# Two local-attention layers and their feed-forwards, written as one unrolled stream of 32 tile steps

## The reference

```python
x = x + _L0_xattn_ref(ctx_768, layernorm(x), mask, ...)   # A: 2 heads of 64, 256 + 256 keys
x = x + _L0_ffn_ref(layernorm(x), ...)                    # B: two layers of the following
x = x + _L1_xattn_ref(layernorm(x), ctx_768, ...)         # C: 8 heads of 64, 256 keys
x = x + _L1_ffn_ref(layernorm(x), ...)                    # D: gated feed-forward with fake quantisation

def _layer(x, wqkv, qs, ksc, wo, lg, lb, w1, b1, w2, b2):  # one layer of B
    q, k, v = split(shift_token(x) @ wqkv)                # 8 heads of 64
    q, k = rotary_xpos(l2norm(q) * qs, l2norm(k) * ksc)
    x = x + local_attention(q, k, v) @ wo
    h = layernorm(shift_token(x)) * lg + lb
    a, g = split(h @ w1 + b1)                             # 2 x 341 columns
    return x + (a * gelu(g)) @ w2 + b2
```

## Time and profile before

| | |
|---|---|
| median of 3 runs | 1018.42 us (1013.97 to 1022.93) |
| span of the profiled execution | 1025.1 us |
| PE busy (share of the span) | 870.8 us (85%) |
| PEld, DVE, ACT, POOL busy | 539.7, 665.1, 539.1, 386.2 us (53, 65, 53, 38%) |
| A, B, C and D in the profiled execution | 0 to 184.7, to 743.7, to 971, to 1025.1 us |

### The profile page before, as it was taken

The page is one execution under the profiler, slowest core; times in us unless marked ns, Lnnn a source line. Parts: engine busy times, 40 slices in busy tenths (PEclk is TensorE's granted clock), DMA queues, the critical chain, the costliest instruction groups (busy, mean ns, idle before and its releaser), DMA issues.

```text
span 1025.1 us, 17045 instructions
## 1 busy us (share of the span) xinstructions
PE 870.8 (85%) x4931; PEld 539.7 (53%) x4931; DVE 665.1 (65%) x1935; ACT 539.1 (53%) x1490; POOL 386.2 (38%) x476
## 2 busy tenths in 40 slices
PE   2898889699999998795999999987989999999642
PEld 1344444355565566563555555564656666666411
DVE  3755663467777777554577777765556666667566
ACT  1445552346666666422466666663256566555252
POOL 5634452655555554114565555621000111110102
PEclk9879995769999999998699999999999999999765
DMA  6400000000000000101000000000000000000001
GB/s 187 92 1 1 0 0 0 1 1 1 1 1 0 0 0 1 44 2 24 0 0 0 0 0 0 0 0 0 1 1 1 2 0 0 0 0 1 1 1 41
DMA packets 16492, 10.40 MB, mean 10 GB/s; under 512 B 6612, under 2 KB 15390, under 8 KB 16351
## 3 DMA queue, kind: packets, MB, share of 16 engines
q1 hardware_dynamic: 16446, 9.90, 3.8%
HBM read 8.84 MB, written 1.05 MB: 10 GB/s over the span
## 4 chain that ended last, share of the span: by engine, by line
PE 31%; DVE 11%; issue 5%; ACT 3%; POOL 1%; DVEq 0%; POOLq 0%; ACTq 0%
PE PS L655 8%; PE PS L665 5%; PE PS L685 4%; PE PS L707 3%; PE PS L741 2%; PE PS L759 2%; PE PS L849 2%; DVE mx L1161 2%; PE PS L766 1%; PE PS L749 1%; DVE rsin L1259 1%; DVE ss L1262 1%; PE PS L762 1%; PE PS L858 1%; ACT pb L950 1%
## 5 line engine op out<-in xcount | busy, mean ns | idle before, releaser
L655 PE MATMUL PS<-big 64*128 64x192 f32 (+3 forms) x832 | 216.8, 387 | 0.8 <-ACT big L1004 0.8
L655 PEld LDWEIGHTS PS<-big 64*128 64x128 f32 x832 | 129.0, 196 | 55.8 <-issue 52.2
L1161 DVE TENSOR_REDUCE mx<-PS 128x2 f32<-128x384 f32 (+3 forms) x192 | 122.7, 639 | 39.3 <-PE PS L655 37.7
L541 POOL TENSOR_TENSOR rot<-rot,rsin 128x512 f32<-128x512 f32 x64 | 83.7, 1308 | 162.0 <-DVE rsin L1259 161.9
L741 PE MATMUL PS<-wqkv,hB 128*128 128x512 f32 x192 | 113.8, 693 | 27.9 <-ACT hB L989 18.7
L1009 ACT ACTIVATE pT<-PS 128x512 f32<-128x512 f32 x192 | 115.0, 599 | 20.4 <-PE PS L665 20.4
L685 PE MATMUL PS<-pT,V 128*64 128x128 f32 x1280 | 108.5, 292 | 11.9 <-ACT pT L1009 9.7
L685 PEld LDWEIGHTS PS<-pT,V 128*64 128x64 f32 x1280 | 68.8, 139 | 86.7 <-issue 70.1
L1179 DVE RECIPROCAL rden<-den 128x2 f32<-128x2 f32 (+2 forms) x192 | 31.2, 162 | 117.3 <-ACT pb L950 53.4
L665 PE MATMUL PS<-ident,pb 128*128 128x128 f32 x512 | 88.6, 299 | 3.9 <-DVE pb L1188 3.8
L996 ACT ACTIVATE sq<-PS 128x512 f32<-128x512 f32 x64 | 38.2, 597 | 86.8 <-PE PS L741 86.3
(11 more groups left out here) (217 smaller groups left out, 1596.4 us busy)
## 6 DMA issues: line engine op xcount, KB each, us to landing
wqkv<-in_L_ffn_wqkv SPq DMA_DIRECT2D x2, 768.0 KB, 4.6
out<-x SPq DMA_DIRECT2D x4, 256.0 KB, 2.3
x<-in_x SPq DMA_DIRECT2D x1, 768.0 KB, 5.4
ctxT<-in_ctxT SPq DMA_DIRECT2D x1, 768.0 KB, 7.5
w<-in_L_ffn_w SPq DMA_DIRECT2D x2, 341.0 KB
ctxs<-in_ctx SPq DMA_DIRECT2D x1, 576.0 KB, 6.5
woB<-in_L_ffn_wo SPq DMA_DIRECT2D x8, 64.0 KB, 3.8
x<-in_x SPq DMA_DIRECT2D x1, 256.0 KB, 2.8
```

What stands on the lines that cost most here:

```text
L541: tt(rot[:, m, :], rot[:, m, :], rsin[:, is_q, :], ALU.add).then_inc(sem("B_sum"), 1)
L655: i = mm(bank[:, n * nk:(n + 1) * nk], q, k, start=(ph == "C"), stop=(ph == "C" or n == len(heads) - 1))
L1161: red(m, PS[:, SB + s % 2, 0:nh * nk].rearrange("p (n k) -> p n k", n=nh), AXX, ALU.max) \
```

## The change

Only B is written anew; A, C and D keep their code. The loop over layers, the loop over batches, the units, pieces and the separate feed-forward of B go. In their place every engine has one straight list of 47 steps: tile n (0 to 31: two layers of 16 tiles) enters at step n, and each engine's part of it follows at a fixed lag.

- **Scores.** All 8 heads of a tile stand in two banks at once. Each window of 64 queries meets 128 keys: its own 64 and the 64 before. So a head takes two matmuls of 64 contraction rows, 64 stationary columns and 128 moving ones, 16 per tile, and the two masks are 512 columns each.
- **Softmax.** One maximum over 128x1024, one subtraction of it over 128x1024 (DVE), one exp over 128x1024 (ACT), eight transposes back into the same two banks, one copy of 128x1024 (ACT). Nothing is divided there: V has a 65th column of ones, so that the value sum brings the row sum with it, and DVE divides the 512 outputs.
- **Values.** The turned probabilities are stationary (64 columns), V moves (65 columns), 16 matmuls per tile. The outputs come out by tokens, so four transposes (L870) and a copy are added. The first window's keys are mixed from two tiles by one or two DMAs from SBUF to SBUF (`mixed_values`).
- **q and k.** POOL takes the 16 inverse norms in one power and scales both q and k.
- **Feed-forward.** Group g's steps lie at steps 4g+7 to 4g+13 between the attention's, with one pair of banks for its three up-chunks, so each chunk waits for the gelu and the gate of the one before. The shifted half comes by three DMAs (`shifted_half`), and POOL adds `b2`.
- **Loads.** Both layers' weights are loaded at the start, layer 1's into `xy`, which was free until C. The scales `xeff` of both layers are made in A's last batch.
- PE, ACT and POOL's B parts start when all of `y` is ready; C starts on PE after the last residual of B.

```diff
-            with pe.Fori(0, DEPTH) as layer:
-                pe.wait_ge(sem("ld_wqkv"), layer * 112 + 112)
...
-                attention("B", layer, between=lambda: f_shift(0))
...
+            def b_scores(n):
+                pe.wait_ge(sem("B_qT"), n + 1)
+                pe.wait_ge(sem("B_kT"), n + 1)
+                if n >= 1:
+                    pe.wait_ge(sem("B_pT"), n)
+                j = n % 2
+                for r in range(2):
+                    mm(PS[:, BS + r, :], identb[:], (band_b if j else band_a)[:], start=True, stop=False)
+                for c in range(4):
+                    for w in range(2):
+                        for r in range(2):
+                            rows = slice(r * DH, (r + 1) * DH)
+                            keys = kTB[rows, n // 2 % 2, c, j * P + w * WINDOW:j * P + w * WINDOW + P]
...
+                            i = mm(PS[w * WINDOW:(w + 1) * WINDOW, BS + r, c * P:(c + 1) * P],
+                                   qTB[rows, n % 2, c, w * WINDOW:(w + 1) * WINDOW], keys, start=False, stop=(c == 3))
+            def b_values(n):
...
+                for k, h in enumerate(HEADS):
+                    for w in range(2):
+                        v = vown[:, n % 3, h, :] if w else vmix[:, n % 2, h, :]
+                        i = mm(PS[w * WINDOW:(w + 1) * WINDOW, BO + k // 4, k % 4 * 65:(k % 4 + 1) * 65],
+                               pTB[n % 2][:, k, w * WINDOW:(w + 1) * WINDOW], v, start=True, stop=True)
+            for i in range(LAST_STEP + 3):          # PE; its order within a step
+                up01, up2, down, ft = group_at(i, 11), group_at(i, 12), group_at(i, 13), group_at(i, 10)
...
+                    f_up(up01, 0)
...
+                    b_project(i, 0, BP).then_inc(sem("B_q"), 1)
...
+                    f_down(down)
...
+                    f_up(up2, 2)
...
+                    b_turn_outputs(i - 4)
...
+                    f_turn(ft)
+                if 2 <= i < NT + 2:
+                    b_scores(i - 2)
...
+                    f_up(up01, 1)
...
+                    b_project(i, 1, BP + 1).then_inc(sem("B_k"), 1)
...
+                    b_output(i - 4)
+                if 3 <= i < NT + 3:
+                    b_values(i - 3)
...
+                    b_turn(i + 1)
...
+                    b_turn_qk(i - 1, 1, BP).then_inc(sem("B_qt"), 1)
...
+                    b_project(i, 2, BK).then_inc(sem("B_v"), 1)
...
+                    b_turn_qk(i - 1, 0, BP + 1).then_inc(sem("B_kt"), 1)
+                if 2 <= i < NT + 2:
+                    b_turn_probs(i - 2)
...
+            for i in range(LAST_STEP + 3):          # DVE; POOL and ACT have lists of the same kind
+                if 3 <= i < NT + 3:
+                    b_max(i - 3)
...
+                    f_gate(g, 2)
...
+                    b_residual(i - 5)
...
+                    f_gate(g, 1)
...
+                    b_rotate(i - 1, 0)
+                    b_sum_squares(i - 1, 0)
...
+                    b_divide(i - 4)
...
+                    b_sum_squares(i - 1, 1)
...
+                    f_stats(g)
...
+                    b_rotate(i, 1)
```

More of the change, by code:

```diff
@@ L141, in over_batches, with values_landed, group_at @@
     body(B - 1, 1, "last")
+def values_landed(n):
+    return 16 * (1 + n % 2) * (n // 2 + 1)
+def group_at(i, first):
+    g, r = divmod(i - first, 4)
+    return g if r == 0 and 0 <= g < GROUPS else None
 def wait(eng, sem, value):
@@ L398, in ffn_weights @@
                              "ld_w12")
[L399 to L404, removed]
-            later_loads()
[L406 to L410, removed]
-                sp.wait_ge(sem("y_ready"), layer * B + B + FIRST)
-                ffn_weights(layer)
+                load(lnB[:, layer, 0:1], t_in["L0_ffn_ln_g"][layer].rearrange("(n o) -> n o", o=1), "ld_w12")
@@ new lines, in _ @@
+            pool.wait_ge(sem("ld_w12"), DEPTH * 12 * 16)
+            for i in range(LAST_STEP + 2):
+                if 1 <= i <= NT:
+                    b_add(i - 1, 0)
+                if (g := group_at(i, 12)) is not None:
+                    f_bias(g)
+                if (g := group_at(i, 8)) is not None:
+                    f_copy(g)
+                if 1 <= i <= NT:
+                    b_roots(i - 1)
+                    b_scale(i - 1, 1)
+                    b_scale(i - 1, 0)
+                if (g := group_at(i, 8)) is not None:
@@ L803, in attention @@
                     turn_probs(ph, u, s)
-                    if s == n - 2 and between:
-                        between()
                     if ph != "A" or s % 2:
@@ new lines, in _, with b_tokens, b_square @@
+            act.wait_ge(sem("B_pad"), 2)
+            def b_tokens(n):
+                act.wait_ge(sem("B_xt"), n + 1)
+                at, bank = hB[:, n // 2 % 2], PS[:, BK + 1, 0:P]
+                j = n % 2
+                af(at[0:DH, j * P:(j + 1) * P], bank[0:DH], ACT.Copy)
+                af(at[DH:D, j * P + 1:(j + 1) * P + 1], bank[DH:D], ACT.Copy).then_inc(sem("B_hB"), 1)
+            def b_square(n, w):
+                act.wait_ge(sem("B_%s" % "kq"[w]), n + 1)
+                wait(act, sem("B_ss%d" % w), n)
+                af(sqB[w], PS[:, BP + 1 - w, :], ACT.Square).then_inc(sem("B_sq%d" % w), 1)
@@ L1325, in body @@
                         dve.wait_ge(sem("ln_rstd"), 6)
-                    if ph == "B":
-                        dve.wait_ge(sem("B_rs"), layer * (4 * B) + b * 4 + 4)
+                    if ph == "A" and where == "last":
+                        xpos_scales()
                     for s in range(n):
@@ new lines, in b_residual, with f_stats @@
+            def b_residual(n):
+                dve.wait_ge(sem("B_wo"), n + 1)
+                yt = y[:, n % T, :]
+                tt(yt, PS[:, BP, 0:D], yt, ALU.add).then_inc(sem("B_ya"), 1)
+            def f_stats(g):
+                dve.wait_ge(sem("B_fc"), g + 1)
+                dve.wait_ge(sem("B_fs"), (g + 1) * 48)
+                for j in range(4):
+                    i = nc.vector.bn_stats(bstf[:, j, :], hs[:, j, :])
+                then(i, "B_fbn", g + 1)
+                for j in range(4):
+                    i = nc.vector.bn_aggr(mvh[:, j, :], bstf[:, j, :])
+                i.then_inc(sem("B_hst"), 1)
```

711 lines of the change are left out of this document (397 added, 314 removed).

## The result

| | before | after |
|---|---|---|
| median, us | 1020.67 (4 runs, 1013.97 to 1033.21) | 895.09 (4 runs, 893.98 to 902.80) |
| span of the profiled execution, us | 1025.1 | 892.5 |
| B, from its first block on PE to C's first | 559.0 | 432.9 |

The ratio is 0.879 with an interval of 0.873 to 0.886: faster, by 126 us. Now and then an execution runs longer at a lower granted clock throughout (the worst here is one of an experiment, 1156.9 us at 0.65, beside 943.4 at 0.91), and the ratios leave such executions out. The forecast was 931 in a range of 890 to 990. The range held; the gain was 1.4 times the 87 us forecast.

The account below looks back on a forecast made before the run. PE was taken as the bound. 32 tiles at 11.4 (365), feed-forward 67, fill 15 and drain 18 make B 465 us, ending 89 earlier; less 2 for seams, 87 saved: 938 profiled, 931 median, range 890 to 990.

Parts of the forecast that it names:

- B's start: First block of B on PE: it waits for all of `y`, finished by POOL, so B begins at 189.5 us.
- the seams: Where B meets A and C: 2 us taken off the 89 us gain, leaving 87.
- The mechanism: In B, PE bounds the stream: 13.5 us per tile with feed-forward, against at most 9.7 on any other engine.
- PE per tile, 10.6 and 0.8 for waits: Attention in B: PE's blocks sum to 10.6 us per tile, plus 0.8 idle: 11.4, against 13.7 before.
- The rival of the four quarters: Scores and values in B both run at their lower ends, 1.6 us less per tile: 886 us; chance 0.13.
- The feed-forward, 8.4 per group: Feed-forward within B's stream: PE works 8.4 us for each of eight groups, 67 us in all.
- Fill and drain, 33: Start and end of B's stream: 15 us to fill, paid once instead of twice, and 18 to drain.
- The DMAs, costed at nothing: Transfers of mixed V and the shifted half in B land in time, at no cost; 2 us late per group costs 16.
- POOL, DVE, ACT: Other engines in B, per tile with feed-forward: POOL 9.7, DVE 9.3, ACT 8.2 us, below PE's 13.5.
- The rival of late chains: Power, table loads or the probabilities' copy are late in B, some 1.6 us per step: +50, 981 us; chance 0.17.
- The drains: PE must empty between array quarters, so 64 small-matmul rows per tile pay 0.17 each: +237, 1168 us; chance 0.05.
- The clock: Short waits keep the granted clock low: B's 465 us become 552, no gain, at 0.79; chance 0.02 within 1%.

Follow-up runs that it names:

- the version without the stall: Feed-forward statistics, their inverse root and application one step later than in the changed kernel, nothing else: median 854.35 us, 0.834 of the kernel before, B 386.4 us.

## Why the prediction was right, and where it was off

On the profiled executions 938 was forecast and 892.5 came. Of the 45.5 us, 13.3 are B's start (189.5 forecast, 176.2 measured) and 32.1 its length (465 against 432.9); the 2 us taken off for the seams were right (283.4 behind B in place of 281.4). By the prediction's own steps:

- **The mechanism: right.** PE's work per tile sets the stream, and no other engine does. Without the stall PE is busy 99% of a period, and changes of 0.49, 0.75 and 1.46 us per tile came out as 13.5 to 14.2, 23.8 and 46.9 us.
- **PE per tile, 10.6 and 0.8 for waits: too high.** A plain step is 8.73 us. Scores were taken at 1.9 and measured 1.03, close to the lower bound of 0.9. Values were taken at 1.6 and measured 1.08, close to theirs of 1.0. The waits of 0.8 were not there. These three make 2.2 of the 2.7; the remaining half microsecond is spread over blocks that had rows. Eight transposes start 0.87 before the next block (207.97 to 208.84; forecast 0.98), and a projection 0.86 (208.84 to 209.70; forecast 0.955). In the third step, which has no wait, the four transposes of the outputs and both masks take 1.02 from start to start (1.19 forecast). Over 32 tiles: 279 us in place of 365.
- **The rival of the four quarters: it came true.** The choice was "the value rows' 0.053", since no row of before showed both halves of the rows at work. I gave that 0.55 and the overlap 0.13. The runs that reorder the score rows show that it is the alternation of both halves that gives 1.03: with one half it is 1.52, not far from the 1.9 forecast for just that. The rival's own time of 886 was only 9 us off, but partly by luck: it foresaw no stall and a later start. The bounds were right; the choice between them was not.
- **The feed-forward, 8.4 per group: right.** In the version without the stall a group's period is 341.40-297.96=43.44 us (start of a step to the same step of the next group); less 4x8.73 this leaves 8.5.
- **Fill and drain, 33: right to 6 us.** 386.4-279.4-8x8.5=39.0 for both and for the lower clock in them.
- **The DMAs, costed at nothing: wrong, and the largest single error.** "The shifted half has some 3 us before DVE asks" was right (3.9), but the data came 11.0 us after the residual: 1.4 until SyncE issued the transfer, and most of the rest at 18 GB/s. The price named for a miss, "2 us late once per group would be 16", has the right form; it was 7.1 late in the group above and cost 46.5 us. What was missing was the pace of the transfer, with 0.08 of the DMA engines at work, and its place in SyncE's list. No row of before could have shown the pace, since that kernel has no transfer from SBUF to SBUF; but a range of one price only, 2 us, was too narrow for an operation without a row. It is this step that hides the overlap's gain: 279+68+39+46.5 gives the 432.9 measured.
- **POOL, DVE, ACT: right.** The power over 16 elements takes 2.95 us (3.0 forecast), the maximum over 1024 columns 1.22 (1.24), exp over 1024 1.06 (1.0). "Table loads with slack behind them" was right: removing them changed nothing.
- **B's start: off by luck.** A's rows on PE are the same (x656 in both; DVE has 19 more, the scales `xeff`). B waits there for all of `y`, as forecast (its first L810 waits 5.05 us for POOL), but A was granted a clock of 1.00 from 80 to 160 us, where the profiled execution of before had 0.96 and 0.89 in the two halves of that stretch and 0.56 from 160 us to B. In the nine kernels' profiles B's start lies between 176.0 and 193.5, which holds the forecast: at 176.0 to 177.5 in the four where A's clock was 1.00 from 80 to 160 us, and at 184.5 to 193.5 in the five where it was not.
- **The rival of late chains: no.** A plain step waits 0.33 for the copy of the probabilities, and the ones behind it not at all. **The drains: no.** 64x64 rows at 0.032 leave no room for one. **The clock: no, but its mechanism is there.** B's clock was 0.93 before and is 0.93 after, far from the 0.79 of no gain. But the stalls did take some of it: without them it is 0.97, worth 14.3 us.

Read as a whole, a forecast of 931 missed 86 us of gain in PE's tiles (work and waits) and a loss of 46.5 in a stall; the two errors have opposite signs, and the range held for that reason as much as for its width. With the stall gone the median is 854, below the range's lower end of 890: that the range held was luck in good part.

## What to carry to other kernels

When small matmuls are tiled over quarters of the array, order the loops so that neighbouring rows differ in both halves; the same 32 rows took 1.03 us so, 1.52 with two halves alternating, and 2.49 in turn. Before an unrolled stream is called finished, look through the in-order list of the second-busiest engine for an instruction that waits for a DMA: what stands behind it waits too, and one step's delay of that instruction was worth 40 us here. For a DMA on the path, look in the windows at the share of the DMA engines beside the GB/s: 127 KB went at 18 GB/s here, with 0.08 of them busy, and the issue behind it on the same queue stood for 6.49 us meanwhile.

## What the runs showed of the hardware

- Two transfers of about the same size from SBUF to SBUF went at 180 GB/s (64 pieces of 2080 bytes, 64 partitions, 0.82 of the DMA engines busy) and at 18 (508 pieces of 256 bytes, 127 partitions, 0.08 busy). In "DMA: Bandwidth & Descriptors", Why small descriptors are slow (HBM only), the Trainium skill says that transfers from SBUF to SBUF don't suffer the penalty of small pieces. For 256 bytes the rows agree: 18 GB/s at 0.08 is as much for each busy engine as 180 at 0.82. For 32 bytes they don't: 5 GB/s at 0.10. What keeps the share so low stays open; a shift over 128 partitions wasn't tried.
- SyncE issued the slow transfer in 0.74 us, but its next issue, of two pieces, took 6.49, and 3.07 and 0.95 where the slow transfer was shorter. The one after that took 0.56 in all three. What holds the issue wasn't tried.
- Score rows of a single quarter still follow each other at 0.078 us where rows of 64 contraction rows took 0.135 with the same 128 moving columns but in the 64*128 form. I did not separate whether the narrower stationary side or the order of the halves does this.
- Stalls of some 4.5 us once in 50 took the granted clock of B from 0.97 to 0.93, worth 14 of the 46.5 us; behind one of them, of 4.48 us, the clock was 0.51 for the next 3.15 us.
